# Two-layer cross-attention on one core: every pair of heads turned on VectorE in 32 by 32 blocks, the blocks exchanged directly between partitions, keys made in block order

## What is computed

```python
def attention(q, k, v, mask):                      # 16 heads
    s = einsum('bqhd,bkhd->bhqk', q, k) * scale
    s = where(mask, very_negative, s)
    return einsum('bhqk,bkhd->bqhd', softmax(s), v)

x = ln0(attention_A(x Wq, ctx Wk, ctx Wv) Wo + bo + x)
x = ln1(x + attention_B(x, x, x, mask_SxS) o)
x = ln2(x + attention_C(x, ctx, ctx) co)
x = ln3(x + relu(x lin1) lin2)
```

## Time and profile before

| | |
|---|---|
| runs | 1845.80, 1817.69 and 1824.84 us, median 1824.84 |
| profiled execution | 1826.15 us |
| its span, first to last instruction | 1824.3 us |
| mean granted TensorE clock | 0.985 of 2.4 GHz |
| PE busy | 1719.5 us (94%) |
| DVE busy | 1269.6 us (70%) |
| ACT, POOL busy | 1190.3 us (65%), 990.9 us (54%) |
| DMA | 324.12 MB, 178 GB/s over the span |

### The profile page before, as it was taken

One profiled execution on the slowest core, in us unless ns is written; L12 is line 12 of the kernel. 1 busy time (PEld: TensorE's weight loads), 2 busy tenths in 40 slices (PEclk: granted clock), 3 DMA queues, 4 the chain that ended last, 5 costly groups with the idle time before them and its releaser, 6 DMA issues.

```text
span 1824.3 us, 36986 instructions
## 1 busy us (share of the span) xinstructions
PE 1719.5 (94%) x11328; PEld 1287.7 (71%) x11328; DVE 1269.6 (70%) x4778; ACT 1190.3 (65%) x3985; POOL 990.9 (54%) x1030
## 2 busy tenths in 40 slices
PE   7999999999999999999999999999999999998887
PEld 5776677777777677777777777677777777776556
DVE  3465667786868668686776868678686867667763
ACT  3364766667676666767666676766667677566752
POOL 3252655657465464746556474555657565455742
PEclk9999999999999999999999999999999999998899
DMA  7432327585766758576585757658575766613010
GB/s 167 143 106 84 107 67 230 172 273 161 238 204 200 245 170 272 161 244 206 178 266 181 249 159 236 209 181 280 173 251 163 226 223 182 202 59 139 30 58 12
DMA packets 227521, 324.12 MB, mean 178 GB/s; under 512 B 31744, under 2 KB 196352, under 8 KB 219136
## 3 DMA queue, kind: packets, MB, share of 16 engines
q1 hardware_dynamic: 224208, 321.75, 55.5%
q10 hardware_dynamic: 3120, 0.01, 0.1%
HBM read 170.69 MB, written 151.00 MB: 176 GB/s over the span
## 4 chain that ended last, share of the span: by engine, by line
PE 77%; DVE 6%; DMA 5%; ACT 5%; SPq 5%; issue 2%; POOL 0%; POOLq 0%; DVEq 0%
PE ps_g L681 45%; PE ps_t L824 10%; PE ps_t L847 8%; PE ps_s L800 8%; ACT prob L930 3%; PE ps_av L800 3%; DMA prob_b<-p_kept 3%; PE ps_av L847 3%; DVE prob L1105 2%; DMA p_kept<-blocks 2%; SPq L593 1%; PE ps_g L687 1%; DVE res_ln L1081 1%; DVE prob_b L1136 1%; SPq L576 1%
## 5 line engine op out<-in xcount | busy, mean ns | idle before, releaser
L1229 POOL TENSOR_TENSOR prob<-prob,recip 128x512 f32<-128x512 f32 x768 | 788.4, 1049 | 670.5 <-DVE recip L1115 670.4
L930 ACT ACTIVATE prob<-prob,ext 128x256 f32<-128x256 f32 x1536 | 757.2, 499 | 11.7 <-DVE ext L1105 11.5
L940 ACT ACTIVATE prob_t<-ps_t 128x512 f32<-128x512 f32 x384 | 226.3, 594 | 398.1 <-PE ps_t L824 397.3
L824 PE MATMUL ps_t<-ident,prob 128*128 128x128 f32 x1920 | 304.6, 283 | 7.6 <-DVE prob_b L1136 5.4
L930 ACT ACTIVATION_READ_ACCUMULATOR prob<-prob,ext 128x1 f32 x1536 | 295.5, 192 | 0.0
L824 PEld LDWEIGHTS ps_t<-ident,prob 128*128 128x128 f32 x1920 | 216.9, 142 | 94.2 <-issue 51.6
L1105 DVE CUSTOM_DVE_ANT_0 prob<-ps_s,mask_a 128x256 f32<-128x256 f32 x392 | 145.3, 421 | 88.3 <-PE ps_s L800 70.6
L1127 DVE STREAM_TRANSPOSE blocks<-prob 128x512 f32<-128x512 f32 x288 | 183.9, 676 | 3.2 <-POOL prob L1229 2.3
L1105 DVE CUSTOM_DVE_ANT_0 prob<-ps_s,zero 128x256 f32<-128x256 f32 x392 | 144.4, 418 | 45.3 <-PE ps_av L800 37.3
L1105 DVE CUSTOM_DVE_ANT_0 prob<-ps_s,mask_b 128x256 f32<-128x256 f32 x368 | 135.9, 417 | 24.5 <-PE ps_s L800 14.8
L800 PE MATMUL ps_s<-k_ctx,q 64*128 64x256 f32 x784 | 144.8, 402 | 7.3 <-DVE ext L1105 3.0
(11 more groups left out here) (116 smaller groups left out, 2980.9 us busy)
## 6 DMA issues: line engine op xcount, KB each, us to landing
p_kept<-blocks SPq DMA_DIRECT2D x576, 128.0 KB, 2.4
prob_b<-p_kept SPq DMA_DIRECT2D x144, 512.0 KB, 3.4
k_parts_C<-k_hl SPq DMA_DIRECT2D x64, 256.0 KB, 3.1
k_parts_B<-k_hl SPq DMA_DIRECT2D x64, 256.0 KB, 3.1
q_parts_B<-q_hl SPq DMA_DIRECT2D x64, 256.0 KB, 3.5
k_B<-k_parts_B SPq DMA_DIRECT2D x16, 1024.0 KB, 7.6
q_B<-q_parts_B SPq DMA_DIRECT2D x16, 1024.0 KB, 7.7
q_parts_C<-k_hl SPq DMA_DIRECT2D x64, 256.0 KB, 4.7
```

The source lines that it names most:

```text
L824: last = nc.tensor.transpose(two(ps_t[e])[:, kt, qt * P:(qt + 1) * P], src[:, e, qt, kt * P:(kt + 1) * P], ident[:, :])
L930: last = nc.scalar.activation(tile, tile, ACT.Exp, bias=ext[:, slot, e, t:t + 1], scale=-1.0, accum_out=sums[:, slot, e, t:t + 1])
L940: nc.scalar.activation(prob_t[:, e], two(ps_t[e]), ACT.Copy).then_inc(copied_second, 1)
L1229: nc.gpsimd.tensor_tensor(rows, rows, recip[:, slot, e].unsqueeze(2) .to_broadcast([P, TT, TOK]), ALU.mult).then_inc(normed[s], 1)
```

## The change

All 384 pairs are turned by DVE, in one transpose of 128x1024 a pair that reads `prob` from end to end. PE's transposes for the weights, the banks `ps_t`, `prob_t` and their copies on ACT and DVE are gone. The two pairs of a quad share a slot of `blocks` (ring of 2), and when both are there four DMAs carry 1 MB directly from SBUF to SBUF into `prob_b`. The DRAM tensor and the reading back are gone.

With this, key r of block g lands at partition 4r+g and no longer at 32g+r. So the keys are permuted: A's, B's and C's key projections read their moving operand in that order (`keys_out`, a step of 4 elements), and the masks are permuted before the launch.

W moves one place later (`LAG` = 4). Score banks are four everywhere, two pairs, so PE may start a pair once the pair two before has been taken. Keys of B and queries of B and C also go directly from SBUF to SBUF in 8 DMAs each; keys of C still go through DRAM. The job `v` goes to ACT. `P_RING` is 3. `x_tok` is gone: the residual input is loaded straight into `res_ln0`. The tables of jobs are written anew for the new lag.

```diff
-P_RING = 4
-LAG, BLOCKS = 3, 2
+P_RING, B_RING, T_RING = 3, 2, 2
+LAG, BLOCKS = 4, 2
...
     def advance(self, jobs):
...
-        if older(BLOCKS, 0, True):
-            steps.append(("D",) + older(BLOCKS, 0, True))
-        if older(BLOCKS + 1, 0, True):
-            steps.append(("L",) + older(BLOCKS + 1, 0, True))
-        turn = older(LAG, 0, False) or older(LAG, 1)
-        if turn:
-            steps.append(("T0",) + turn)
+        if g - BLOCKS in pairs:
+            steps.append(("D",) + pairs[g - BLOCKS])
         steps.extend(jobs)
-        weigh = older(LAG + 1, 1)
+        old = pairs.get(g - LAG - 1)
...
-        if turn:
-            steps.append(("T1",) + turn)
...
-        ("A", 1): [dma("k", "B"), job("qs"), ln("ln1"), job("v", 0)],
+        ("A", 1): late + [job("qs"), dma("k", "B")],
...
-        ps_s = [bank("ps_s0"), bank("ps_s1")]
-        ps_t = [bank("ps_t0"), bank("ps_t1")]
+        ps_s = [bank(f"ps_s{i}") for i in range(4)]
...
+            def exchange(body, step):
+                quad = body.quad(step)
+                sp.wait_ge(flipped, 2 * quad + 2)
+                if quad >= T_RING:
+                    (_, s0, p0, _), b0 = body.pair_at(2 * (quad - T_RING))
+                    sp.wait_ge(weighed[s0], count(b0, QUADS, p0 // 2 + 1))
                 for q in range(4):
+                    sp.dma_start(prob_b[:, quad % T_RING, q].rearrange("p j x -> p (j x)"),
+                                 blocks[q * SLOT:(q + 1) * SLOT, quad % B_RING].rearrange("r g j x -> r g (j x)")
+                                 ).then_inc(landed[quad % T_RING], 16)
...
+            def spread_keys(b):
+                sp.wait_ge(taken["ks"], count(b, 1, 1))
+                home_free("B", b, "B")
+                for part in range(PARTS):
+                    for e in range(2):
+                        row = HALF * e + DH1 * part
+                        sp.dma_start(k4["B"][row:row + DH1].bitcast(F32), k_hl[:, part % 2, e]
+                                     ).then_inc(spread_k["B"], 16)
...
+            def keys_out(ps, w, first, src):
+                for m in range(2):
+                    c = (first + m) * P
+                    last = product(ps[:, m, :].rearrange("p (k g r) -> p k g r", k=TT, r=SLOT),
+                                   [w[:, d, c:c + P] for d in range(DT)],
+                                   [src[:, d, :].rearrange("p (k r g) -> p k g r", k=TT, r=SLOT) for d in range(DT)])
+                return last
...
-                past = body.earlier(step, 1, lambda x: x[0] == "S")
+                past = body.earlier(step, 2, lambda x: x[0] == "S")
...
+                    return nc.tensor.matmul(out.rearrange("p (t q r) -> p t q r", t=TT, r=SLOT), w,
+                                            by_query[j][:, e, kt], start=kt == 0, stop=kt == TT - 1, **tile)
...
             def turn_blocks(body, step):
...
-                src = prob[:, body.slot(step, P_RING)].rearrange("p e t (k g r) -> p k (e t) g r", k=TT, r=SLOT)
-                out = blocks[:, :, :].rearrange("p g (k x q) -> p k x g q", k=TT, q=SLOT)
-                for kt in range(TT):
-                    last = nc.vector.transpose(out[:, kt], src[:, kt])
-                last.then_inc(flipped, 1)
+                if quad >= B_RING and p % 2 == 0:
+                    dve.wait_ge(landed[(quad - B_RING) % T_RING], 64 * ((quad - B_RING) // T_RING + 1))
+                src = prob[:, body.slot(step, P_RING)].rearrange("p e t (k g r) -> p (e t k) g r", k=TT, r=SLOT)
+                out = blocks[:, quad % B_RING, :, p % 2].rearrange("p g (m q) -> p m g q", q=SLOT)
+                nc.vector.transpose(out, src).then_inc(flipped, 1)
```

More of the change, by code:

```diff
@@ L158, in schedule @@
     if present == {"x", "a"}:
-        after = {place: [x for x in jobs if x[1:3] not in (("res0", 0), ("load", 0))] for place, jobs in after.items()}
+        after = {place: [x for x in jobs if x[1:3] not in (("res0", 0), ("x_in", 0), ("mask_in", 0), ("v", 2), ("v", 3))] for place, jobs in after.items()}
         after["A", 0] = [job("k", 1)] + after["A", 0]
-        head += [res("res0", 0), io("load")]
+        after["A", 7] = [job("v", 2)]
+        head += [res("res0", 0), io("mask_in")]
     if present == {"x"}:
@@ L165, in schedule @@
     steps += here(head)
-    line = Line(steps, carried, blocked)
+    line = Line(steps, carried)
     for o in order:
@@ L173, in schedule, with last_schedule @@
     if not closed:
-        for _ in range(LAG + 1):
-            line.advance([])
+        for i in range(LAG + 1):
+            line.advance([job("v", 3)] if present == {"x", "a"} and i == 1 else [])
         steps += here(wo + os + first)
     return steps
-def last_schedule(carried, blocked):
+def last_schedule(carried):
     steps = []
@@ L478, in place, with score_bank @@
             return 4 * (p // 4) + 2 * (p % 2) + (p // 2) % 2
-        def score_bank(body, step, e):
-            if body.full:
-                return (ps_s + [ps_av])[(2 * body.place(step) + e) % 3]
-            return ps_s[e]
-        def weigh_bank(body):
-            return ps_t[1] if body.full else ps_av
+        def score_bank(body, step, i):
+            return ps_s[(2 * body.place(step) + i) % 4]
         def bodies():
@@ L503, in _, with load_mask @@
         def _(sp):
-            def load(body, step):
+            def load_mask(body, step):
                 b = body.batch(step)
@@ L584, in spill @@
[L584 to L600 removed]
+                    for e in range(2):
+                        row = HALF * e + DH1 * part
+                        sp.dma_start(q4[home][row:row + DH1].bitcast(F32), parts[:, part // 2, e]
+                                     ).then_inc(spread_q[s], 16)
@@ L783, in scores @@
                 else:
[L784 to L785 removed]
+                    n = 16 * SPREADS if s == "B" else 16
+                    pe.wait_ge(spread_k[s], count(b, n, n))
+                    pe.wait_ge(spread_q[s], count(b, 16 * SPREADS, 16 * SPREADS))
                     home = HOME.get(step[3], s)
                     q, k = q4[home][:, place(p), :], k4[home][:, place(p), :]
[L788 removed]
+                past = body.earlier(step, 2, lambda x: x[0] == "S")
                 if past:
                     (_, s0, p0, _), b0 = past
[L792 to L796 removed]
+                    pe.wait_ge(masked[s0], count(b0, HEADS, 2 * p0 + 2))
                 for t in range(TT):
@@ L932, in exps @@
                     last.then_inc(exped[s], 1)
-            def evac_turned(body, step, e):
-                if step[2] % 2 == 0:
-                    return
-                quad = body.quad(step)
-                act.wait_ge(turned, 2 * (quad + body.turned_so(quad + 1, False)) + e + 1)
-                nc.scalar.activation(prob_t[:, e], two(ps_t[e]), ACT.Copy).then_inc(copied_second, 1)
             def evac_weighed(body, step):
@@ L1095, in extremes @@
                 slot = body.slot(step, P_RING)
+                n = body.place(step)
+                if n >= P_RING:
+                    dve.wait_ge(flipped, n - P_RING + 1)
                 if s == "A" and p == 0:
```

370 lines of the change are left out of this document (138 added, 232 removed).

## The result

The changed kernel takes 2144.4 us (median of 4 runs, 2138.4 to 2150.7), the kernel before 1823.7. The ratio is 1.178, its interval 1.173 to 1.182. The forecast was 1685 us, in a range of 1630 to 1815, and faster. The range does not hold the time.

What follows compares the result with a forecast made beforehand. PE was taken to bound the kernel, busy 97% of full bodies. Gains of 93.6 us in full bodies, 30 in the first and 20 in the last stretch, 144 in all, took 1826.15 to 1682, stated as 1685, range 1630 to 1815.

Steps and rivals of the forecast that it cites:

- PE's relief: Full bodies: dropping 24 groups of transposes saves PE 12.4 us a body, from 103.4 to 91.0.
- DVE's side: Full bodies: 24 transposes of 1.16 us add 13.4, `v` leaving saves 2.7; DVE goes from 79.1 to 89.8 us.
- I take no cost: Key products' stepped read on PE: taken as free, upper bound 10.4 us a body; rival at half pace, 1801 us, chance 0.20.
- How the two meet: Full bodies: PE and DVE even out over three places, 97.2 plus 1.8 for late exchanges, 99 us a body.
- no evening out: Rival, full bodies: PE and DVE wait for each other at each place; body 106, time 1766, chance 0.14.
- The exchange: SP: four issues 2.6 us, landing 2.4 to 4.8, so 5 to 7.4 from transpose to weighing, covered by 12.3.
- My sign for it: PE waiting for `prob_b<-blocks` more than 5 us a body would show SP's queue.
- The rival on SP's queue: 16 DMAs ahead delay exchanges at four places a body; body 116.6, time 1894, chance 0.07.
- The clock: Last stretch: the granted clock, 0.94 there, may not recover; no separate price.
- The first bodies: First stretch, 270.7 us: 48 pairs save 49 us of PE, of which 30 us was taken as gain.
- The last pairs: Last stretch, 228.3 us: same arithmetic, but DVE sets the pace for the last 24 pairs; gain of 20 us.
- the signs that I had named for being wrong: A full body staying above 103 us, or PE's instructions becoming slower.

Runs made afterwards that it cites:

- e11: e9 with one of the four DMAs of each exchange, the rest of the turned blocks staying zero; 1862 us.
- e1: Changed kernel with its key products reading their moving operand in order, so keys are not permuted; 1998 us.
- e2: Kernel before with only its key products reading the moving operand at a step of 4 elements; 1988 us.
- e6: Changed kernel with the key permutation moved from PE's moving operand to the ACT and DVE instructions that take products out of PSUM; 2023 us.
- e5: Changed kernel with key products in order, spreads of keys and queries issued by ACT, and a quarter of each exchange; 1954 us.
- e4: Changed kernel with one of the four DMAs of each exchange, the other turned blocks staying zero; 2034 us.
- e9: Changed kernel with keys permuted out of PSUM, spreads on ACT, weighed quads before exponents on ACT, x2T and x3T transposes last in their places; 1996 us.
- e3: Changed kernel with the 24 DMAs a batch that spread B's keys and B's and C's queries issued from ACT's queue; 2131 us.
- e12: Changed kernel with keys permuted out of PSUM, spreads on ACT, weighed quads before exponents on ACT, and weighing one place earlier; 2134 us.

## Why the prediction was wrong

**PE's relief.** Right. The transposes went, and nothing else on PE changed its count. In e11, with the keys in order and the clock at 0.95, PE is busy 96.7 us a body. An estimate from that clock: a mean of 0.95 is a tenth of the 107.4 us at the lower of the two levels, half of full, which costs 5 us and leaves 91 to 92, the 91.0 of the forecast.

**DVE's side.** Right to 1.5%: 88.5 us a body for 89.8.

**"I take no cost" for the key products.** Wrong, and the largest single loss that the runs isolate: 9.3 us a body in e1, 10.4 in e2. The bound was right and the choice between the bounds was not. I had a row that pointed to the cost (a POOL copy), and the Trainium skill's rule (Advanced Engine Details and Errata, SBUF Cachelines) that one hit a line is too few. I set against them an argument from PE's column time, which no row of a stepped read supported. The rule stands: the key products' pace halved. On PSUM the Trainium skill (Advanced Engine Details and Errata, section PSUM Cachelines) says that any non-contiguous pattern slows matmuls significantly. e6 has only ACT and DVE read PSUM with a step, and ACT's reads do not suffer, 470 for 467 ns.

**"How the two meet": evened out over three places, 99 us a body.** Wrong. e5 has the three disputed costs off and takes 114. Four score banks let PE run ahead of the extremes, but the table has four or five points in a body at which PE reads what DVE and ACT made in the place before. There the lead goes, and PE waits for chains across engines. Before, the same waits were 20.6 us for the last A quad and 4.0 for a normed tile in all full bodies; in e5 they are 79.6 and 57.4. An average over work says nothing of them. My reading is that PE, then the latest engine, hid them by its own lateness; the table of jobs is new as well, and no run tried the relief with the old one. The rival "no evening out", body 106, went the right way from 99 and was still short.

**The exchange.** Wrong. I rated it as covered for all but 1.8 us a body, from issue and landing times of transfers to DRAM. The direct one takes 0.77 and 4.5 us where I had 0.65 and 2.4 to 4.8, so the size was not the fault, the cover was: three quarters of it cost 6 us a body (e4) and 110 us in all, and 134 once other waits are gone (e9 to e11). My sign for it, PE waiting over 5 us a body for `prob_b<-blocks`, did not come: PE waits 2.9 there and 4.7 for C's scores, which stand behind exchanges in SP's queue. The rival on SP's queue named this place and a time of 1894, and had a chance of 0.07. Its jam at C's queries happened, but moving the spreads away gave 13 us, so that mechanism alone does not carry its 118.

**The clock.** I mentioned it for the last stretch only. It fell to 0.91 in the full bodies. PE's work is 91 us a body by the forecast, 10.4 with the keys makes 101.4, and PE was busy 109.6. So some 8 us a body, by this difference, are matmuls at the lower of the two levels after idle time. One place in the changed kernel shows it, the output projection's sixteen instructions after a wait of 3.59 us and sixteen like them just behind, with the granted clock of both stretches (0.60 and 1.00):

```profile
1070.72 5.99 PE L639 MATMUL ps_g<-wo,k_ctx 128*128 128x256 f32 x16 [3.59 <-ACT k_ctx L876]
...
1077.07 3.72 PE L639 MATMUL ps_g<-wo,k_ctx 128*128 128x256 f32 x16
```

```profile
1070.70:1076.60 5.90, 5.88 (x16) 4.56 (x16) 1.68 (x6) 1.89 (x8) 2.04 (x2) 0.60 1.04 334
1077.00:1080.70 3.70, 3.70 (x20) 2.96 (x16) 2.69 (x10) 2.07 (x8) 1.75 (x2) 1.00 0.93 233
```

**The first bodies.** Forecast 30 us less, measured 67 more. They had no turning by blocks before, so no DMA stood between scoring and weighing. Now the first exchange stands behind the weights in SP's queue. PE and SP there:

```profile
16.58 1.13 PE L766 MATMUL ps_s<-k_ctx,q 64*128 64x256 f32 x8 [0.64 <-ACT k_ctx L850]
...
28.27 3.87 PE L639 MATMUL ps_g<-c_t,wk 128*128 128x256 f32 x8
31.95 1.91 PE L639 MATMUL ps_g<-wv,c_t 128*128 128x256 f32 x8
...
42.78 1.13 PE L766 MATMUL ps_s<-k_ctx,q 64*128 64x256 f32 x8 [0.98 <-issue]
68.91 0.69 PE L780 MATMUL ps_av<-prob_b,v 128*64 128x256 f32 x2 [25.00 <-DMA prob_b<-blocks]
```

```profile
54.25 5.88 SPq L469 DMA_DIRECT2D mask_u<-mask_BxSxS_bf  x1
60.17 1.26 SPq L557 DMA_DIRECT2D prob_b<-blocks  x2
```

The pairs were scored from 16.58 us on, the mask's load was held until 60, the first exchange was issued at 60.17 and PE weighed at 68.9 after 25 idle us. This is read from the trace. No run took it away: e4 with its quarter of an exchange still stands 21.3 us there. The key products are another part, the first stretch of e1 is 28 us shorter.

**The last pairs.** Forecast 20 us less, measured 6 more, with the granted clock at 0.81 where it was 0.94. I had named the clock as a doubt and given it no price. e1 takes 10 us off this stretch; the rest is not separated.

Together, a body: 99 of forecast, 10 for the keys, 8 for the clock, and 10 for waits on exchanges and between dependent steps make 127. The last of these is what remains and not a measurement. The parts are not independent, as e3, e9 and e12 show. Both of the signs that I had named for being wrong came: a body above 103, and slower instructions on PE.

One slip beside these: ACT lost 384 copies of `ps_t` and not the 240 that I wrote. It changes nothing, ACT was not the bound.

## What to carry to other kernels

When the engine that trails all others is relieved, list every place where it reads what the others have just made, and follow each chain back through the queues; the sum of loads holds only if none of them is tight. Put a permutation where an instruction reads PSUM to take a product out, not into the moving operand of a matmul (shown here for float32 and a step of 4). Taking one wait out of several in a row may show little, so take several out together before judging.

## What the runs showed of the hardware

A float32 moving operand with a step of 4 elements halved PE's pace: 3.69 us for eight instructions of 256 columns against 1.84 for eight plain ones in the same run, and 164 us for 768 of them with everything else equal (e2). The same step on PSUM reads cost ACT nothing, 470 ns for 467 (e6); DVE's addition took 480, as long as another instruction of its size without the step. After 3.59 us of idle time PE's granted clock was 0.60 of full over the next sixteen matmuls, which took 5.99 us where sixteen like them at the full clock took 3.72. DMAs between partitions of SBUF took 0.77 us each to issue at 256 KB and 4.5 to land, where those of 128 KB to DRAM took 0.44 and 2.4 in the kernel before (all of these are medians); with a quarter of the exchange they took 0.55 and 3.6.
